# Gated message stage of a graph network: two norms scaled on ScalarE, norm sums in PSUM, destination norm one turn earlier

## The reference, cut to what matters

```
h = jnp.maximum(_layernorm(x), 0.0)          # at the sources and at the destinations
x_t = leaky_relu(h @ W1n + b1n, 0.1) @ W2n + b2n
e_t = ...                                    # two-layer product of the edge features
msgs = x_t[src] * e_t
aggregated = segment_sum(msgs, dst)
out = h + aggregated * res_w
x = x + (out - mean(out)) * rsqrt(var(out) + EPS) * gamma + beta
```

## Time and profile before

| what | us |
|---|---|
| median of 3 runs | 5482.65 (5470.95 to 5494.29) |
| the profiled execution, its own time | 5440.1 |
| its span, first to last instruction | 5438.3 |
| first index gather of the stage that the change touches | starts at 3281.3 |
| last `x2` of the stage | starts at 3868.1 |

### The profile page before, as it was taken

How to read it: one execution, slowest core, us unless ns; L and a number is a source line. 1 busy time by engine, 2 the same in 40 slices (tenths; PEclk the granted TensorE clock), 3 DMA queues, 4 the chain that set the end, 5 groups by cost and what they waited for, 6 DMA issues and landing times. The chain is left out here.

```text
span 5438.3 us, 65663 instructions
## 1 busy us (share of the span) xinstructions
PE 3357.0 (62%) x13753; PEld 1886.9 (35%) x13801; DVE 3749.1 (69%) x6348; ACT 2194.7 (40%) x4957; POOL 3702.8 (68%) x3739
## 2 busy tenths in 40 slices
PE   8998688856665777577736885777443335441110
PEld 3443455634443333244424553444222212221000
DVE  8876789957775444489987896999544457674231
ACT  0000678843332111166737883444212146662110
POOL 7776775767776777577724436777477767775776
PEclk9999899986777565599978998999655556665555
DMA  4543997753333333466624442333344422222221
GB/s 62 76 52 54 147 196 223 234 179 100 105 105 81 80 84 80 112 191 202 206 93 127 137 137 70 94 96 93 92 135 134 124 72 78 78 71 85 77 81 51
DMA packets 562758, 611.16 MB, mean 112 GB/s; under 512 B 306536, under 2 KB 310760, under 8 KB 560916
## 3 DMA queue, kind: packets, MB, share of 16 engines
q1 hardware_dynamic: 342965, 474.39, 28.1%
q0 software_dynamic: 115712, 104.00, 9.3%
q10 hardware_dynamic: 104000, 31.92, 5.2%
HBM read 357.91 MB, written 303.78 MB: 122 GB/s over the span
## 5 line engine op out<-in xcount | busy, mean ns | idle before, releaser
L1144 POOL DMA_INDIRECT l_got<-d_x,l_near x1176 | 1172.2, 997 | 456.7 <-issue 348.9
L856 PE MATMUL ps<-hot_lo,hot_w 128*128 128x512 bf16 x2304 | 507.4, 380 | 15.7 <-DVE hot_lo L792 13.2
L1144 POOL DMA_INDIRECT p_got<-d_h,p_near x392 | 373.7, 953 | 170.1 <-issue 114.4
L2545 POOL DMA_INDIRECT out<-fi_res,fi_near x392 | 375.3, 957 | 164.0 <-issue 119.2
L729 POOL DMA_INDIRECT d_pos<-place,near x392 | 398.6, 1017 | 123.8 <-issue 117.9
L1144 POOL DMA_INDIRECT p_got<-d_sums,p_near x392 | 376.0, 959 | 147.1 <-issue 118.3
L1144 POOL DMA_INDIRECT p_got<-d_ext,p_near x392 | 381.8, 974 | 134.4 <-issue 116.4
L1152 POOL DMA_INDIRECT ln_xd<-d_xt,idsE x304 | 286.9, 944 | 129.3 <-issue 89.6
L856 PEld LDWEIGHTS ps<-hot_lo,hot_w 128*128 128x128 bf16 x2352 | 230.6, 98 | 292.9 <-issue 16.9
L1349 DVE TENSOR_TENSOR_SCAN p_sums<-same,p_sums,ps 65x512 f32<-65x512 f32 (+1 forms) x196 | 239.8, 1263 | 118.8 <-PE ps L1456 112.3
L417 PE MATMUL ps<-ident,fi_sums 128*128 128x128 f32 x196 | 53.2, 427 | 411.5 <-DVE fi_sums L1332 401.9
(11 more groups left out here) (427 smaller groups left out, 10372.5 us busy)
## 6 DMA issues: line engine op xcount, KB each, us to landing
l_xd<-d_x SPq DMA_DIRECT2D x147, 256.0 KB
d_ext<-ln_ext SPq DMA_DIRECT2D x98, 264.0 KB
d_xt<-in_x_wide ACTq DMA_DIRECT2D x49, 520.0 KB
ln_x<-in_x SPq DMA_DIRECT2D x98, 256.0 KB
d_h<-ln_hb SPq DMA_DIRECT2D x98, 256.0 KB, 2.9
d_x<-ln_x SPq DMA_DIRECT2D x98, 256.0 KB
lb_x<-d_x SPq DMA_DIRECT2D x49, 512.0 KB
d_x<-lb_x SPq DMA_DIRECT2D x49, 512.0 KB
```

The costliest lines, as they stand in the source:

```text
L856: last = nc.tensor.matmul(bank(h), hot_w[:, r, k], hot_lo[:, r, 512 * h:512 * h + 512], start=False, stop=False)
L1144: nc.gpsimd.indirect_dma_start(out=out[:, q], out_offset=None, in_=source, in_offset=bass.IndirectOffsetOnAxis(ap=ids[:, q:q + 1], axis=0) ...
L2545: nc.gpsimd.indirect_dma_start(out=out, out_offset=bass.IndirectOffsetOnAxis(ap=near[:, r, q:q + 1], axis=0), in_=res[:, r, q], in_offset= ...
```

## The change

`Norm` for `d` and `o` becomes `NormScaled`: the scalings `hd` and `xn` leave DVE and become eight ACTIVATEs each on ACT. The vectors `sum` of all three norms and `rstd` of norm `s` move to PSUM bank 5, which the stage didn't use. The piece `dests` is cut in two: norm `d` now stands in list 2 (group t-2), and a new piece `added`, with `o1`, in list 3 (group t-3). The ACT piece `dests` moves to list 2 with it. The lists of SP and POOL, and the four slots of `xd`, stay as they are.

```
-    def __init__(self, sem, t, name):
+    def __init__(self, sem, t, name, small=None):
...
+        if small is not None:
+            self.sum = small
...
-        norm_s, norm_d, norm_o = (Norm(sem, t, "l1_" + n) for n in ("s", "d", "o"))
+        norm_s = Norm(sem, t, "l1_s", small=bank(5))
+        norm_d, norm_o = (NormScaled(sem, t, "l1_" + n, bank(5)[:, 2 * S + S * k:3 * S + S * k]) for k, n in enumerate(("d", "o")))
...
                 def dests(i, r, g):
                     dve.wait_ge(x_in[r], i * 16 + 16)
-                    yield from norm_d.dve(nc, dve, g, 0, xd[:, r])
-                    nc.vector.scalar_tensor_tensor(out=hd[:], in0=norm_d.xc, scalar=0.0, in1=spread(norm_d.rstd),
-                                                   op0=ALU.max, op1=ALU.mult).then_inc(m["hd_done"], 1)
+                    yield from norm_d.dve(nc, dve, g, r, xd[:, r])
+
+                def added(i, r, g):
                     yield 9
-                    dve.wait_ge(m["hd_done"], g + 1)
+                    dve.wait_ge(norm_d.scaled, g + 1)
                     dve.wait_ge(m["back"], g + 1)
...
-                    yield from norm_o.dve(nc, dve, g, 0, o1[:])
-                    after(dve, m["xn_t"], g)
-                    nc.vector.tensor_tensor(xn[:], norm_o.xc, spread(norm_o.rstd), ALU.mult).then_inc(m["xn_done"], 1)
+                    yield from norm_o.dve(nc, dve, g, r, o1[:])
...
-                ring_loop(dve, GROUPS, [sources], [], [sums_of], [dests], [normed], [result])
+                ring_loop(dve, GROUPS, [sources], [], [sums_of, dests], [added], [normed], [result])
...
-                    hold(pe, m["xn_done"], g + 1)
+                    hold(pe, norm_o.scaled, g + 1)
...
-                    yield from norm_d.act(nc, act, g, 0)
+                    yield from norm_d.act(nc, act, g, r, hd, ACT.Relu, m["o1_done"])
...
-                    yield from norm_o.act(nc, act, g, 0)
+                    yield from norm_o.act(nc, act, g, r, xn, ACT.Copy, m["xn_t"])
...
-                ring_loop(act, GROUPS, [sources], [b], [], [dests], [normed], [residual])
+                ring_loop(act, GROUPS, [sources], [b], [dests], [], [normed], [residual])
```

More of the change, by code:

```diff
@@ L2109, in gated_messages @@
         hid = [t(f"l1_hid{k}", [P, G_ROWS])[:] for k in (0, 1)]
-        norm_s, norm_d, norm_o = (Norm(sem, t, "l1_" + n) for n in ("s", "d", "o"))
-        names = ("hn_done", "hn_t", "hf_done", "mm1", "hid_done", "mm2", "msg_done", "carry", "back", "hd_done",
-                 "o1_done", "xn_done", "xn_t", "xf_done", "residual", "x2_done")
+        norm_s = Norm(sem, t, "l1_s", small=bank(5))
+        norm_d, norm_o = (NormScaled(sem, t, "l1_" + n, bank(5)[:, 2 * S + S * k:3 * S + S * k]) for k, n in enumerate(("d", "o")))
+        names = ("hn_done", "hn_t", "hf_done", "mm1", "hid_done", "mm2", "msg_done", "carry", "back",
+                 "o1_done", "xn_t", "xf_done", "residual", "x2_done")
         m = {n: sem("l1_" + n) for n in names}
```

## The result

| what | us |
|---|---|
| median of 4 runs of the changed kernel | 5527.68 (5523.29 to 5529.94) |
| median of 4 runs of the kernel before, on the same chip | 5481.59 (5470.95 to 5494.29) |
| ratio, 95% interval | 1.0085 (1.0071 to 1.0098) |
| profiled execution after, its own time, span | 5523.29, 5521.5 |

The change costs 46 us of 5482 (39 to 54 by the interval). The forecast was 5533 us, with 5508 to 5566 as its range. The two profiled executions lie 83 us apart; that of before is 41 us under its own median, and 25 us of the difference stand ahead of the touched stage, which begins at 3306.1 here and at 3281.3 before. So the stage is compared by its own length: from the first gather to the last `x2` it takes 3945.7 - 3306.1 = 639.6 us, against 586.8, which is +52.8.

What follows compares the result with a forecast made beforehand. DVE was taken to bound the touched stage, with DVE-stalled gathers close behind. +48.6 (late load) - 2 (start) + 4 (end) = +50.6 us on 5440.1 gives 5490.7; with runs 0.8% above that execution, 5533 us, range 5508 to 5566.

Steps and rivals of the forecast that it cites:

- The term that decides: Touched stage: `xd`'s load, released by `x2`, is needed almost at once; turn 12.26 us instead of 11.13, +48.6 us over 43.
- PSUM operands at nothing: DVE's three centrings and `hn` reading PSUM vectors: between nothing and 0.24 us a turn, taken as nothing.
- the wait that the forecast took off as 0.20: DVE's wait for ACT's square in each turn, expected to vanish because DVE comes there late: 0.20 us.
- Copies at nothing: Sixteen copies on ACT, 3.92 us a turn; their loop of 11.10 us fits in 12.26, so costed at nothing.
- The first rival: Load lands early, so the loop through ACT and PE sets the turn at 11.10 us: 5484 us, chance 0.08.
- The faster rival: Neither loop closes, so POOL's bare gathers set the turn at 9.95 us: 5433 us, chance 0.05.
- two limits close together: Touched stage before the change: limited by DVE's own work and by gathers that DVE's work holds up; turn 11.13 us.
- The reading of the long gather: POOL's gather starting during DVE's row of centrings takes 2.64 us, ending as one of them ends; otherwise 0.94 to 0.96.
- The slower rival: PE loses its clock, lengthening transposes and the product with `w1n` by some 2.5 us: 5563 us, chance 0.12.
- The ends: Stage start before `x2` of group 0 gains 2 us; the last five turns after group 43 cost 4 us more.
- the -2 for the turn from which norm `d` is absent: Third of the last five turns, without norm `d`: about 2 us shorter.

Runs made afterwards that it cites:

- e4: Kernel before with the load of `xd` waiting for one `x2` more, nothing else of the change: ratio 1.0194 to the kernel before.
- e2: Changed kernel plus a second, separately loaded tile from which `x2` reads its rows, so the load for norm `d` is released earlier: ratio 0.9981 to the kernel before.
- e1: Changed kernel with two buffers for `hd`, so the first eight copies need not wait for `o1`: ratio 1.0090 to the kernel before.
- e6: Changed kernel with norm `d` back in list 3 and on DVE; only norm `o` ends in copies on ACT: ratio 0.9946 to the kernel before.
- e3: Changed kernel with both two buffers for `hd` and a second tile for `x2`: ratio 0.9908 to the kernel before.
- e5: Kernel before with sums and reciprocals of all three norms in the free PSUM bank, nothing else of the change: ratio 0.9990 to the kernel before.
- e7: Changed kernel with `x2` right behind the scan instead of at the end of the turn: ratio 1.0033 to the kernel before.
- e8: Changed kernel with `x2` right behind the scan and two buffers for `hd`: ratio 0.9981 to the kernel before.

## Why the prediction was right

**The turn.** The term that decides was the loop from `x2` through the load back to `x2`: 9.21 + 0.15 + 2.9 = 12.26 us forecast, 9.11 + 0.17 + 2.88 in the turn shown, 12.27 in the mean. DVE idled for 114.8 us in 45 waits before the sum over `xd`, where 110 in 45 were named:

```profile
its engine sat idle before it (us, times) until:
  DMA l_xd<-d_x: 114.8, 45
```

That the mean agrees to 0.01 us is in part luck: DVE's part came out 0.10 us under the forecast, and the wait, 114.8 / 45 = 2.55 us, 0.10 over. That this wait is the cause, and not only a place where time shows, rests on both directions: put into the kernel before, it costs 1.9% (e4); taken out of the change, it gives 1.0% back (e2).

**PSUM operands at nothing.** Right: the three centrings take 0.680 to 0.681 us in the median, against 0.681 to 0.685 before. The 0.10 us that DVE's part was under the forecast lie elsewhere, at the product with the edge values:

```profile
3570.79 0.75 DVE L2166 SCALAR_TENSOR_TENSOR ps<-ps,vecs,l_et 128x512 f32<-128x512 f32 x1
```

From its start to that of the first sum of squares DVE needed 3571.74 - 3570.79 = 0.95 us before and 3606.40 - 3605.74 = 0.66 after, so the wait that the forecast took off as 0.20 was worth 0.29.

**Copies at nothing.** Right while the load is late: sixteen copies take 3603.12 - 3599.20 = 3.92 us, as forecast, the last root is done at 3608.93 and the reciprocal follows the scan at 3609.69. ACT's loop had 0.76 us to spare in this turn, where 1.16 was forecast. Two buffers for `hd` gained nothing (e1). The first rival, that ACT's loop sets the turn, is what follows when the load is early: 10.85 us in e2, where 11.10 was worked out. The rule of the Trainium skill, "ScalarE: Activation LUTs", section "Rules for kernel authors", to keep such work on VectorE is not borne out here. By the rows eight copies take 1.92 us on ACT from their start to the next, and the scaling on DVE 0.60. Still e6 is 0.5% and e3 0.9% faster than the kernel before, in which ACT was busy for 47% of this stretch and DVE for 98%.

**The faster rival.** Its turn of 9.95 us exists, e3 has it, but only with both loops opened. In one step the reading of before was wrong: "two limits close together". Taking the gathers' stalls away alone gained nothing that can be told (e5). DVE waited for gathered rows only 4.5 us of 360, as much as for ACT's squares in the turns with a slow product of PE, a limit that the prediction didn't see in the kernel before. The reading of the long gather was wrong in a detail too: it doesn't end as a centring ends. It ends at 3571.69, and the last centring at 3570.88; the product with the edge values, at 3570.79 + 0.75 = 3571.54, ends between them. The cause of the stalls agrees with the Trainium skill, "SBUF — State Buffer", section "Who interferes with whom": in e5 the only change is that the small vectors lie in PSUM, so that the centrings and scalings have one SBUF operand instead of two, and no gather of the stage takes more than 0.979 us. In the changed kernel it is 0.980.

**The slower rival.** PE kept its clock: 0.92 granted in the stretch, 0.93 before. The product with `w2n` took 5.1 to 6.7 us instead of 3.67 in 24 of the 43 turns (16 before), but behind the load there was room for it: these turns last 12.0 to 12.8 us, and the others 12.1 to 12.6.

**The ends.** The start of the stage, from the first gather to `x2` of group 0, gained (3377.0 - 3306.1) - (3355.0 - 3281.3) = -2.8 us (forecast -2). The last five turns took 41.1 us against 34.5, +6.6 where +4 was forecast. One by one they are 10.20, 10.59, 8.66, 5.84 and 5.84, against 8.93, 9.10, 7.10, 4.71 and 4.64. The first two, with waits for the load of 3.08 and 2.86 us, grew by 1.27 and 1.49 (forecast 1.9 each), and the last two by 1.13 and 1.20 (forecast 1.3 each). The step that failed is the -2 for the turn from which norm `d` is absent: it grew by 1.56. No load is awaited there; what makes it longer is the copies on ACT, which the forecast counted only in the last two:

```profile
3927.47 2.00 ACT L246 ACTIVATE l_xn<-l_o_xc,l_o_rstd 128x64 f32<-128x64 f32 x8
...
3929.62 1.09 PE L411 MATMUL ps<-ident,l_xn 128*128 128x128 f32 x4 [2.93 <-ACT l_xn L246]
...
3930.74 0.60 ACT L2259 ACTIVATE l_xf<-ps 128x512 f32<-128x512 f32 x1 [1.27 <-PE ps L411]
...
3931.24 0.62 ACT L238 ACTIVATE l_o_sq<-l_o_xc 128x512 f32<-128x512 f32 x1
...
3931.89 0.69 DVE L226 TENSOR_REDUCE l_o_var<-l_o_sq 128x8 f32<-128x512 f32 x1 [4.51 <-ACT l_o_sq L238]
```

DVE waits 4.51 us for the square of norm `o`, which stands on ACT behind `xf`; `xf` waits for PE's transposes, and these for the last copies.

**The total.** -2.8 + 43 x (12.27 - 11.13) + 6.6 = +52.8 in the profiled executions, forecast +50.6, measured +46 between the medians.

## What to carry to other kernels

A ring of four slots gives slack only by the distance between its first reader and its last: before moving the first reader a turn earlier, count the turns from the release of a slot to the next read of it, and price zero turns at a whole load. Work that moves to an idler engine pays only if its inputs and its output buffer are free when that engine is; look for the one buffer that puts it behind the engine it was meant to relieve. To take away what holds an engine up is no gain if another wait takes its place: test the cause and the price apart.

## What the runs showed of the hardware that was not expected

PE's granted clock did not follow its busy share. In the same 360 us (3420 to 3780) the kernel before had PE busy for 284.11 us at a clock of 0.93, e5 287.14 at 0.92, e7 only 259.98 at 1.00, and e2 273.53 at 1.00; the changed kernel had 267.57 at 0.91. What differs is how long PE stood still before the product with `w2n`: at most 1.7 us in e2 and e7, up to 3.2 in the kernel before, 3.3 in the changed one and 2.7 in e5, where the product after the wait of 2.71 us took 6.67 us, and the one after 1.60 took 3.67. Between them stand e3 (longest wait 2.0, clock 0.99), e6 (2.2, 0.98) and e8 (2.7, 0.94). So the versions with the shortest pauses also run nearly all of the stage at the upper of the two levels, 2.4 GHz. The pause is not all: e1, with up to 4.4, was granted 0.92, no less than the changed kernel, e4, with up to 5.5, 0.88, and in e5 other products took 3.67 after the same 2.71. That the pause does it was not tried by itself.
